# Q2 of the second group by seven 256x256 products: making its weights a group earlier, and the last product's later

## The chip, the cores and the metric

The kernel runs on 1 core of a Trainium2 chip. The metric is the device time of one execution in microseconds (us), as the median of several runs. Lower is better. TensorE (PE) multiplies, VectorE (DVE) and ScalarE (ACT) work on vectors, GpSimd (POOL) sets up, and SyncE (SP) issues nearly all transfers.

## What is computed

`x` holds 64 items of 64 rows by 1024 (4096 rows of 1024 in all). Each item is first multiplied by one of 16 small matrices, then goes through a gated low-rank layer with 64 experts of rank 16, and is added to `x`:

```python
def cond(x, condition, weights):
    return jnp.einsum('bct,bcd->bdt', x, weights[condition])

def ffn(x, A, B, Wr):                      # xf: 4096 rows of 1024
    scores = xf @ Wr.T
    top_vals, top_idx = jax.lax.top_k(scores, 16)
    G = jnp.zeros((N, 64)).at[jnp.arange(N)[:, None], top_idx].set(softmax(top_vals))
    h = jnp.einsum('nd,krd->nkr', xf, A)
    return 2 * jnp.einsum('nkr,kdr->nd', h * G[:, :, None], B)

out = x + ffn(cond(x, cond, W), A, B, Wr)
```

With A and B laid flat these are two products of 4096x1024 by 1024x1024, with gates and a softmax over the 16 best of 64 scores between them.

## The kernel before

**Numbers.** Everything is fp32. For TensorE an operand is split into a high and a low part in a faster type (`fp32r`): ScalarE casts the high part (`hi`, a CAST), VectorE subtracts it from the source to get the low part (`lo`). Three matmuls (high by high, high by low, low by high) stand for one.

**Groups and products.** The 4096 rows are worked in four groups of 1024 (`s` = 0 to 3, `NS`). In each, both large products are done in seven block products instead of eight (Strassen's scheme in Winograd's form). The first half of a group makes P2, P1, P5, P3, P6, P7, P4 (`FIRST`, m = 0 to 6), each in four tiles (j = 0 to 3) of twelve matmuls, one bank of `Pb` per tile. The text calls them tiles 0 to 27 of the group: tile 4m + j. ScalarE copies the results of P2, P1, P5 and P3 out of their banks, VectorE adds up P1, P6, P7 and P4 (`drain_first`). For s > 0 it does this two banks at a time, after the second and the fourth tile. The next product may write a bank only after that. The second half makes Q2, Q1, Q6, Q7, Q4, Q5, Q3 (`SECOND`).

**Products of 256x256.** Some of the products of the second half are themselves done in seven products of 256x256 blocks (`TWO`, by group). Such a product takes 84 matmuls of 256 columns (`two`, line 693) instead of 48 of 512 (`second`, line 674). It needs seven combinations of its input instead of four parts (`FORMS`; four of them are sums by `sums_two`, all seven are split into high and low), and seven combined weights instead of four. Before, Q4 (m = 4) and Q3 (m = 6) are done so from the second group (s = 1) on, Q2 (m = 0) from the third (s = 2) on.

**Made weights.** The seven combined weights of such a product are made once, in the shadow of TensorE's work, from raw blocks of B that lie in SBUF, are stored to `Wd` in HBM, and are loaded from there like all other weights. `MADE_AT` gives the tile at which each of the seven is made and `MADE_IN` the group. At such a tile ScalarE casts the high part into a staging place (`made_hi`), VectorE subtracts the low part (`made_lo`) and after the second, third and fourth does one, two and one sums on the raw blocks in place, and SyncE stores the place at the following tile (`made_store`). A staging place can be cast into again only when its store has landed (`stored`). Before, the weights of Q4 are made in the second half of the first group, those of Q3 at tiles 0, 2, 4, 6, 12, 13, 15 of the second group from the block in `raws[2]` (part of `BR`), those of Q2 at tiles 0 to 6 of the third group, from the same place, which is loaded again with B[0, 0] at tile 18 of the second group. The staging places are the two halves of `xc` (elsewhere the places of x on its way to the small products) and the two halves of `u`.

**Who waits for whom.** The order on each engine is written out by hand in the order of tiles, and each engine works strictly in it. For one tile ScalarE does: the high splits for the next product, `made_hi`, the softmax pieces and score copies, the copy of the banks. VectorE does: the low splits, `made_lo`, the sums T1 to T4 (`sum_t3` at tile 13), the pieces of top 16 (`top_a`, `top_b`, `top_c`), the gates (`gated`), the drain. SyncE does: the weight load for nine tiles ahead (`weights_load`), the store of a made weight, the loads of x for the output (`q_load`, tiles 8 to 15), and at tiles 16 and 20 the small matrices. TensorE turns the gates (`T<-idn,G`) before tiles 12 and 20, when VectorE has finished them. All transfers but a few at the start are issued by SyncE and run on one queue.

## Time and profile before

| | before |
|---|---|
| time, median of 3 runs | 710.89 us (710.61 to 710.94) |
| the profiled execution | 710.62 us, of it span 708.7 us |
| PE busy | 703.5 us (99%), granted clock 1.00 |
| DVE busy | 551.6 us (78%) |
| ACT busy | 274.3 us (39%) |
| transfers | 202.89 MB, mean 286 GB/s |

The span is the time from the first to the last instruction that the profiler recorded; the time of an execution has some 1.9 us more around it. The busy share of an engine is an average over all stages. The granted clock is that of TensorE as a share of full speed. The four groups begin at 9.6, 196.8, 371.1 and 544.6 us, and their second halves at 105.9, 282.1, 456.4 and 630.0.

### The profile page before, as it was taken

Reading aid. Unit: us, or ns where it says so; the run is one execution under the profiler, and the core shown is the slowest. Engines: PE = TensorE matmul, PEld = TensorE weight load, DVE = VectorE, ACT = ScalarE, POOL = GpSimd, SP = SyncE. Lnnn points to the kernel's source line nnn. Section 1 sums busy time; section 2 is a strip of 40 time slices with the busy share of each in tenths; the row PEclk is TensorE's granted clock in tenths of the full one; section 3 lists DMA queues with packets and bytes.
Section 4 is the critical chain, followed back from the end, with each engine's and each line's share of the span. In section 5 each row is a group of like instructions: output and inputs, shape, how many; then the busy total and the mean of one; then the engine's idle time right before and its main releaser. Section 6 shows DMA issues by size and latency. Waiting matters only on the chain.

```text
span 708.7 us, 10694 instructions
## 1 busy us (share of the span) xinstructions
PE 703.5 (99%) x3698; PEld 605.1 (85%) x3698; DVE 551.6 (78%) x991; ACT 274.3 (39%) x505; POOL 1.6 (0%) x6
## 2 busy tenths in 40 slices
PE   9999999999999999999999999999999999999998
PEld 8888888888888888888998888898999888888897
DVE  5898999997757796866675868897677296889985
ACT  5675553535436441133333642232333363222220
POOL 0000000000000000000000000000000000000000
PEclk9999999999999999999999999999999999999999
DMA  9976689747899988476899974967679787565686
GB/s 321 406 296 277 216 282 393 284 184 289 337 381 399 324 328 276 173 239 209 326 331 415 364 293 161 311 248 269 221 295 372 264 304 265 180 232 192 234 322 238
DMA packets 63671, 202.89 MB, mean 286 GB/s; under 512 B 10050, under 2 KB 12738, under 8 KB 62978
## 3 DMA queue, kind: packets, MB, share of 16 engines
q1 hardware_dynamic: 61842, 199.06, 76.3%
q10 hardware_dynamic: 1776, 3.15, 1.3%
q8 instruction: 30, 0.49, 0.3%
q14 instruction: 23, 0.19, 0.1%
HBM read 145.03 MB, written 57.15 MB: 285 GB/s over the span
## 4 chain that ended last, share of the span: by engine, by line
PE 98%; DVE 1%; issue 0%; POOL 0%; DVEq 0%; POOLq 0%
PE Pb L654 43%; PE Pb L687 31%; PE Pb L708 10%; PE Cb L636 8%; PE S L719 4%; PE T L726 1%; PE T L767 0%; PE T L773 0%; DVE Q L1031 0%; PE Pb L670 0%; PE Cb L732 0%; DVE Cq L1031 0%; PE T L732 0%; PE S L732 0%; DVE Op L1031 0%
## 5 line engine op out<-in xcount | busy, mean ns | idle before, releaser
L654 PE MATMUL Pb<-Op,Wt 128*128 128x512 f32 x960 | 231.6, 391 | 0.0
L654 PEld LDWEIGHTS Pb<-Op,Wt 128*128 128x128 f32 x960 | 178.9, 188 | 36.6
L687 PE MATMUL Pb<-Wt,Op 128*128 128x512 f32 x684 | 165.4, 392 | 0.0
L687 PEld LDWEIGHTS Pb<-Wt,Op 128*128 128x128 f32 x684 | 127.0, 188 | 25.9 <-DVE Op L1031 0.4
L1031 DVE TENSOR_TENSOR Q<-Pb,Q 128x512 f32<-128x512 f32 (+1 forms) x114 | 100.9, 901 | 34.9 <-issue 23.5
L855 ACT COPY R<-Cb 128x512 f32<-128x512 f32 x60 | 35.1, 588 | 131.2 <-PE Cb L636 131.0
L1031 DVE TENSOR_TENSOR Op<-R,Op 128x512 fp32r<-128x512 f32 x97 | 64.2, 684 | 27.6 <-ACT Op L805 27.6
L654 PE MATMUL Pb<-Ox,Wt 128*128 128x512 f32 x324 | 81.7, 390 | 0.0
L654 PEld LDWEIGHTS Pb<-Ox,Wt 128*128 128x128 f32 x324 | 60.5, 188 | 12.4
L687 PE MATMUL Pb<-Wt,Ox 128*128 128x512 f32 x276 | 69.5, 391 | 0.0
L708 PE MATMUL Pb<-Wt,Op 128*128 128x256 f32 x516 | 65.5, 284 | 0.3
L708 PEld LDWEIGHTS Pb<-Wt,Op 128*128 128x128 f32 x516 | 63.6, 191 | 1.2 <-issue 0.6
L805 ACT CAST Op<-R 128x512 fp32r<-128x512 f32 x97 | 56.1, 622 | 16.2 <-DVE R L1031 9.3
L805 ACT CAST Op<-Cq 128x512 fp32r<-128x512 f32 x72 | 43.2, 621 | 47.7 <-DVE Cq L1031 32.0
L687 PEld LDWEIGHTS Pb<-Wt,Ox 128*128 128x128 f32 x276 | 51.4, 188 | 10.6 <-DVE Ox L1031 0.2
L1031 DVE TENSOR_TENSOR Op<-Cq,Op 128x512 fp32r<-128x512 f32 x72 | 48.6, 682 | 14.8 <-ACT Op L805 14.8
L1031 DVE TENSOR_TENSOR Cq<-Pb,Cq 128x1024 f32<-128x1024 f32 (+1 forms) x40 | 40.2, 1006 | 24.7 <-issue 16.6
L997 ACT COPY Cq<-Pb 128x1024 f32<-128x1024 f32 (+1 forms) x40 | 33.8, 844 | 44.4 <-issue 39.8
L636 PEld LDWEIGHTS Cb<-wbd,xc 128*128 128x128 f32 x384 | 46.4, 191 | 1.6
L636 PE MATMUL Cb<-wbd,xc 128*128 128x128 f32 x384 | 46.7, 275 | 0.0
L1031 DVE TENSOR_TENSOR Cq<-Cq,SG 128x512 f32<-128x512 f32 x64 | 43.2, 683 | 0.0
L1031 DVE TENSOR_TENSOR R<-R 128x512 f32<-128x512 f32 (+2 forms) x29 | 38.5, 1327 | 0.0
(102 smaller groups left out, 575.0 us busy)
## 6 DMA issues: line engine op xcount, KB each, us to landing
Wt<-Wd SPq DMA_DIRECT2D x192, 512.0 KB, 5.5
Wd<-Wt SPq DMA_DIRECT2D x56, 512.0 KB, 4.8
Q<-in_x SPq DMA_DIRECT2D x32, 512.0 KB, 5.4
xc<-in_x SPq DMA_DIRECT2D x24, 512.0 KB, 4.9
out<-Q SPq DMA_DIRECT2D x8, 1024.0 KB, 4.5
out<-Q SPq DMA_DIRECT2D x13, 512.0 KB, 6.1
BR<-in_B SPq DMA_DIRECT2D x4, 1024.0 KB, 7.8
Wd<-xc SPq DMA_DIRECT2D x8, 512.0 KB, 7.6
```

Of the source, the lines that this page charges most:

```text
L636: t = e.matmul(Cb[:, b, 128 * c:128 * c + 128], src[:, 512 * a + 128 * c:512 * a + 128 * c + 128], wbd[:, i, :], start=True, stop=True)
L654: t = e.matmul(Pb[:, j, :], Wt[:, k, a, 128 * c:128 * c + 128], part((USES1[m], s, c), z), start=fresh and (c, a, z) == (0, 0, 0), stop=(c ...
L687: t = e.matmul(Pb[:, i, :], part((USES2[m], s, c), a)[:, 128 * i:128 * i + 128], Wt[:, k, z, :], start=fresh and (c, a, z) == (0, 0, 0), s ...
L708: t = e.matmul(Pb[:, BANK2[k], 256 * i:256 * i + 256], part((USES2[m], s, k), a)[:, c, 128 * i:128 * i + 128], Wt[:, at, z, 256 * c:256 * ...
L719: t = e.matmul(S[:, :], WrT[:, 4 * a + c, :], part((name, s, c), z), start=begin and (c, z) == (0, 1), stop=not begin and (c, z) == (3, 0))
L726: e.matmul(T[:, 0, :], sS[:, 0:128], sS[:, 0:128], start=True, stop=True)
L805: e.copy(part((name, s, c), 0), source(name, s, c)).then_inc(a_hi, 1)
L855: e.copy(R[:, i // 4, 4 * a:4 * a + 4, 128 * (i % 4):128 * (i % 4) + 128], Cb[:, (v + 1) % 2, :].rearrange("p (c n) -> p c n", n=128)).the ...
L997: e.copy(Cq[:, {"P2": 1, "P1": 0, "P5": 3, "P3": 2}[name], j + 1 - n:j + 1, :], Pb[:, j + 1 - n:j + 1, :]).then_inc(a_prod[name], n)
L1031: e.tensor_tensor(to, one, two, op).then_inc(on, n)
```

## The change

Q2 is done by seven 256x256 products in the second group too (`TWO[1]` gets a 0). Its weights are therefore made in the second group, at tiles 1, 2, 3, 5, 6, 7 and 12, in three staging places: both halves of `xc` and `SG`, which holds the gates. Their raw block B[0, 0] is loaded into `u` near the end of the first group, at step 26 of its second half, instead of into `raws[2]` at tile 18 of the second group. The weights of Q3 are made after them, at tiles 13, 14, 15, 20, 21, 22 and 23, from `raws[2]`, staged in `xc` and `u`. The third group makes no weights. The waits are rewritten to go with this: the copy of the third pair of gates into `SG` waits for the store of Q2's sixth weight.

```diff
--- before.py
+++ after.py
@@ -20,8 +20,8 @@
 SENT = -3.4028234663852886e38
 
 
-TWO = [(), (4, 6), (0, 4, 6), (0, 4, 6)]
-LEVEL = (4, 6, 0)
+TWO = [(), (0, 4, 6), (0, 4, 6), (0, 4, 6)]
+LEVEL = (4, 0, 6)
 
 USED = [[*range(28)] + [n for m in range(7) for n in (
     range(56 + 7 * LEVEL.index(m), 63 + 7 * LEVEL.index(m)) if m in TWO[s] else range(28 + 4 * m, 32 + 4 * m))]
@@ -46,10 +46,9 @@
 SUMS2 = ["t1", "t2", "t3", "t4"]
 
 
-
 MADE = [0, 6, 1, 4, 2, 3, 5]
-MADE_AT = {4: [16, 17, 20, 21, 22, 23, 24], 6: [0, 2, 4, 6, 12, 13, 15], 0: [0, 1, 2, 3, 4, 5, 6]}
-MADE_IN = {4: 0, 6: 1, 0: 2}
+MADE_AT = {4: [16, 17, 20, 21, 22, 23, 24], 0: [1, 2, 3, 5, 6, 7, 12], 6: [13, 14, 15, 20, 21, 22, 23]}
+MADE_IN = {4: 0, 0: 1, 6: 1}
 
 HEAD = [(0, 0, 0), (0, 0, 1), (1, 0, 0), (1, 0, 1), (2, 0, 0), (0, 1, 0), (1, 1, 0), (2, 0, 1), (3, 0, 0), (2, 1, 0),
         (3, 1, 0), (3, 0, 1)]
@@ -361,23 +360,27 @@
         def weight2(m, k):
 
             c, n = [(0, 0), (1, 0), (1, 1), (0, 0), (0, 1), (1, 0), (1, 1)][k]
-            return (u if m == 4 else raws[2])[:, 2 * c:2 * c + 2, 256 * n:256 * n + 256]
+            return (raws[2] if m == 6 else u)[:, 2 * c:2 * c + 2, 256 * n:256 * n + 256]
 
         def made(m, n):
 
 
             if m == 4:
                 return raws[1 - n % 4 // 2][:, 2 * (n % 2):2 * (n % 2) + 2, :].rearrange("p a n -> p (a n)")
-            if n % 4 > 1:
+            if m == 0 and n % 3 == 2:
+                return SG[:, :, :].rearrange("p a n -> p (a n)")
+            if m == 6 and n % 4 > 1:
                 return u[:, 2 * (n % 2):2 * (n % 2) + 2, :].rearrange("p a n -> p (a n)")
-            return xc[:, n % 2, :]
+            return xc[:, n % 3 if m == 0 else n % 4, :]
 
         def made_before(m):
             return 7 * LEVEL.index(m)
 
         def stored(m, n):
 
-            return o_made[n % 4], 16 * (n // 4 + 1 + LEVEL.index(m) * (1 if n % 4 == 3 else 2))
+            k = n % 3 if m == 0 else n % 4
+            ahead = {4: (0, 0, 0, 0), 0: (2, 2, 2, 1), 6: (5, 4, 4, 1)}[m][k]
+            return o_made[k], 16 * (ahead + n // (3 if m == 0 else 4) + 1)
 
         def made_part(m, n, a):
             return made(m, n)[:, 512 * a:512 * a + 512].rearrange("p (c n) -> p c n", n=256)
@@ -496,7 +499,7 @@
 
             def made_store(m, n):
                 e.wait_ge(v_made, made_before(m) + n + 1)
-                e.dma_start(Wd[UNITS + 7 * LEVEL.index(m) + MADE[n]], made(m, n)).then_inc(o_made[n % 4], 16)
+                e.dma_start(Wd[UNITS + 7 * LEVEL.index(m) + MADE[n]], made(m, n)).then_inc(stored(m, n)[0], 16)
 
             def cond_weights(s, half):
                 e.load(which_regs, cnd[0:1, 16 * s + 8 * half:16 * s + 8 * half + 8])
@@ -514,7 +517,8 @@
                     e.wait_ge(p_cond, rows_number(s, i - 2, 0))
                 elif s > 1:
                     e.wait_ge(p_cond, rows_number(s - 1, 6 + i, 0))
-                    e.wait_ge(*stored(6 if s == 2 else 0, 4 + i))
+                    if s == 2:
+                        e.wait_ge(*stored(6, 4 + i))
                 else:
                     e.wait_ge(*operand_used(*LAST_XO[NO + 4 + k]))
                 e.dma_start(xc[:, k, :], xf[128 * n:128 * n + 128, :]).then_inc(l_xc[k], 16)
@@ -561,10 +565,6 @@
                         for k in (6, 0):
                             if s == MADE_IN[k] and step - 1 in MADE_AT[k]:
                                 made_store(k, MADE_AT[k].index(step - 1))
-                        if (s, step) == (1, 18):
-
-                            e.wait_ge(v_made, 14)
-                            e.dma_start(raws[2].rearrange("p a b -> p (a b)"), B[0, 0]).then_inc(l_b[4], 16)
                         if s == 0 and 6 <= step < 10:
                             q = 9 - step
                             e.wait_ge(a_rows, max(rows_all(0, q // 2, 0), rows_all(0, q // 2, 1)))
@@ -597,6 +597,10 @@
                         weights_load(BASE[s] + USED[s].index(UNITS + 7 * LEVEL.index(m) + i if m in TWO[s] else 28 + 4 * m))
                         if s == 0 and step - 1 in MADE_AT[4]:
                             made_store(4, MADE_AT[4].index(step - 1))
+                        if (s, step) == (0, 26):
+
+                            e.wait_ge(v_made, 7)
+                            e.dma_start(u[:, :, :].rearrange("p a b -> p (a b)"), B[0, 0]).then_inc(l_b[4], 16)
                         if s == 0 and m < 6:
                             unit_store(32 + step)
                         k = cond_step(s, m, i)
@@ -806,27 +810,25 @@
 
             def made_hi(m, n):
 
-                if n >= 4:
-                    e.wait_ge(*stored(m, n - 4))
+                if n >= (3 if m == 0 else 4):
+                    e.wait_ge(*stored(m, n - (3 if m == 0 else 4)))
+                elif m == 4:
+                    e.wait_ge(v_wlo, 48 if n < 2 else 52)
+                elif m == 0 and n < 2:
+                    e.wait_ge(l_b[4], 16)
+                    if n == 0:
+
+                        e.wait_ge(v_wlo, UNITS)
+                        for k in range(3, 7):
+                            e.wait_ge(*stored(4, k))
+                    e.wait_ge(p_cond, rows_number(1, 6 + n, 0))
                 elif m == 0:
-
-                    e.wait_ge(*stored(6, n + 4 if n < 3 else 3))
-                    e.wait_ge(l_b[4], 16)
-                    e.wait_ge(v_lo["S4"], split_done("S4", 1, 6))
-                    if n < 2:
-                        e.wait_ge(p_cond, rows_number(2, 6 + n, 0))
-                elif m == 6 and n > 1:
-                    e.wait_ge(v_made, 7)
-                elif m == 6 and n == 0:
-
-                    e.wait_ge(v_wlo, UNITS)
-                    for k in range(3, 7):
-                        e.wait_ge(*stored(4, k))
-                    e.wait_ge(p_cond, rows_number(1, 6, 0))
-                elif m == 6:
-                    e.wait_ge(p_cond, rows_number(1, 6 + n, 0))
+                    for q in range(4):
+                        e.wait_ge(v_gate[q], 4)
+                elif n < 2:
+                    e.wait_ge(*stored(0, (6, 4)[n]))
                 else:
-                    e.wait_ge(v_wlo, 48 if n < 2 else 52)
+                    e.wait_ge(v_made, 14)
                 if n > 2:
                     e.wait_ge(v_wsum, 4 * LEVEL.index(m) + n - 2)
                 e.copy(made_part(m, n, 0).bitcast(F32R), weight2(m, MADE[n])).then_inc(a_made, 1)
@@ -982,6 +984,8 @@
                             h = 2 * s + (m > 3)
                             e.wait_ge(p_gturn, h + 1)
                             if s:
+                                if h == 2:
+                                    e.wait_ge(*stored(0, 5))
                                 e.wait_ge(v_gate[3 if h % 2 else 0], 4 * s)
                             elif h == 0:
                                 e.wait_ge(v_wr, 1)
@@ -1138,9 +1142,8 @@
                 e.wait_ge(v_gate[3], 4 * s + c + 1)
                 if s == 0:
                     e.wait_ge(v_t3, 1)
-                elif s < 3:
-                    e.wait_ge(*stored(6 if s == 1 else 0, 6 if c < 2 else 3))
-                    e.wait_ge(v_lo["S4"], split_done("S4", s - 1, steps(s - 1, 6) - 1))
+                elif s == 1:
+                    e.wait_ge(*stored(6, 6 if c < 2 else 3))
                 else:
                     e.wait_ge(v_lo["S4"], split_done("S4", s - 1, 6))
                 add(s2_place(s, c), Cq[:, 0, c, :], Cq[:, 3, c, :], v_s2, ALU.subtract)
```

**SyncE, end of the first group and tiles 0 to 6 of the second.** `out<-Q` are stores of the output, `Wt<-Wd` weight loads (512 KB), `Wd<-BR`, `Wd<-xc`, `Wd<-u` and `Wd<-SG` stores of made weights. Before:

```order
L499 DMA Wd<-BR 128x1024 [waits v_made] x2
L529 DMA out<-Q 128x2x512 [waits v_out] x2
L490 DMA Wt<-Wd 128x1024 [waits o_t5,o_t7,p_second]
L490 DMA Wt<-Wd 128x1024 [waits o_t6,o_t8,p_second]
L490 DMA Wt<-Wd 128x1024 [waits o_t7,o_t0,p_second]
L490 DMA Wt<-Wd 128x1024 [waits o_t8,o_t1,p_second]
L490 DMA Wt<-Wd 128x1024 [waits o_t0,p_first]
L499 DMA Wd<-xc 128x1024 [waits v_made]
L490 DMA Wt<-Wd 128x1024 [waits o_t1,p_first]
L490 DMA Wt<-Wd 128x1024 [waits o_t2,p_first]
L499 DMA Wd<-xc 128x1024 [waits v_made]
L490 DMA Wt<-Wd 128x1024 [waits o_t3,p_first]
```

and now:

```order
L502 DMA Wd<-BR 128x1024 [waits v_made] x2
L533 DMA out<-Q 128x2x512 [waits v_out]
L603 DMA u<-in_B 128x2048 [waits v_made]
L533 DMA out<-Q 128x2x512 [waits v_out]
L493 DMA Wt<-Wd 128x1024 [waits o_t5,o_t7,p_second]
L493 DMA Wt<-Wd 128x1024 [waits o_t6,o_t8,p_second]
L493 DMA Wt<-Wd 128x1024 [waits o_t7,o_t0,p_second]
L493 DMA Wt<-Wd 128x1024 [waits o_t8,o_t1,p_second]
L493 DMA Wt<-Wd 128x1024 [waits o_t0,p_first]
L493 DMA Wt<-Wd 128x1024 [waits o_t1,p_first]
L502 DMA Wd<-xc 128x1024 [waits v_made]
L493 DMA Wt<-Wd 128x1024 [waits o_t2,p_first]
```

The load of B (`u<-in_B`, 1 MB) stands between the two output stores; the first store of a made weight follows one weight load later than it did.

**ScalarE, tiles 12 to 15 of the second group.** The casts `xc<-BR`, `xc<-u`, `u<-BR` make weights, `S` and `T` are the scores, `Cq<-Pb` copies two banks of P3, the casts from `R` are splits of T2. Before:

```order
L805 CAST Ox<-R 128x512 [waits v_t2,p_first] x2
L832 CAST xc<-BR 128x512 [waits v_wsum,o_made0]
L974 COPY sS<-S 128x512 [waits p_sturn,p_score]
L805 CAST Ox<-R 128x512 [waits v_t2,p_first]
L832 CAST xc<-BR 128x512 [waits v_wsum,o_made1]
L980 COPY sc<-T 128x256 [waits v_top,p_sturn]
L997 COPY Cq<-Pb 128x1024 [waits v_lo_S4,p_first]
L805 CAST Ox<-R 128x512 [waits v_t2,p_first]
L832 CAST u<-BR 128x512 [waits v_wsum,o_made2]
```

and now:

```order
L809 CAST Ox<-R 128x512 [waits v_t2,p_first] x2
L834 CAST xc<-u 128x512 [waits v_wsum,o_made0]
L976 COPY sS<-S 128x512 [waits p_sturn,p_score]
L809 CAST Ox<-R 128x512 [waits v_t2,p_first]
L834 CAST xc<-BR 128x512 [waits o_made0]
L982 COPY sc<-T 128x256 [waits v_top,p_sturn]
L1001 COPY Cq<-Pb 128x1024 [waits v_lo_S4,p_first]
L809 CAST Ox<-R 128x512 [waits v_t2,p_first]
L834 CAST xc<-BR 128x512 [waits o_made1]
L834 CAST u<-BR 128x512 [waits v_made]
```

At tile 12 Q2's last weight is cast into xc's first half; at tile 13, behind the score copy and one split, Q3's first weight is cast into the same half and waits for the store (`o_made0`). Behind it stand the copy of the scores and that of P3's banks.

**VectorE, tiles 13 to 15 of the second group.** `xc<-BR` and `u<-BR` are splits of made weights, `R<-R 128x2048` is the sum T3, then T4; `BR<-BR` are sums on raw blocks. Before:

```order
L1031 TENSOR_TENSOR xc<-BR,xc 128x512 [waits a_made]
L1031 TENSOR_TENSOR R<-R 128x2048 [waits v_lo_y12]
L1031 TENSOR_TENSOR Ox<-R,Ox 128x512 [waits a_hi]
L1031 TENSOR_TENSOR sc<-T,sc 128x256 [waits a_sc]
L1165 MAX m<-sc 128x8 [waits v_top]
L1165 MAX m<-sc 128x8 x3
L1168 TENSOR_SCALAR nm<-m 128x4 [waits v_top]
L1031 TENSOR_TENSOR u<-BR,u 128x512 [waits a_made]
L1031 TENSOR_TENSOR R<-R 128x2048 [waits v_t2]
```

and now:

```order
L1035 TENSOR_TENSOR xc<-BR,xc 128x512 [waits a_made]
L1035 TENSOR_TENSOR R<-R 128x2048 [waits v_lo_y12]
L1035 TENSOR_TENSOR Ox<-R,Ox 128x512 [waits a_hi]
L1035 TENSOR_TENSOR xc<-BR,xc 128x512 [waits a_made]
L1035 TENSOR_TENSOR BR<-BR 128x2x256 [waits v_wlo]
L1035 TENSOR_TENSOR sc<-T,sc 128x256 [waits a_sc]
L1168 MAX m<-sc 128x8 [waits v_top]
L1168 MAX m<-sc 128x8 x3
L1171 TENSOR_SCALAR nm<-m 128x4 [waits v_top]
L1035 TENSOR_TENSOR u<-BR,u 128x512 [waits a_made]
L1035 TENSOR_TENSOR BR<-BR 128x2x256 [waits v_wsum,v_made]
L1035 TENSOR_TENSOR BR<-BR 128x2x256 [waits v_wsum]
```

The sum T4 follows the last of these rows. The split ahead of T3 is now that of Q3's first weight, and between T3 and T4 stand four operations more: a split and a sum at tile 14, two sums at tile 15.

## Rows read from the trace of the kernel before

**Rows 1.** The page's busy times, and the granted clock in 40 slices.
```profile
PE 703.5 (99%) x3698; PEld 605.1 (85%) x3698; DVE 551.6 (78%) x991; ACT 274.3 (39%) x505; POOL 1.6 (0%) x6
...
PEclk9999999999999999999999999999999999999999
```

**Rows 2.** Busy time by stretch: window, length, PE, PEld, DVE, ACT, POOL, clock, DMA, GB/s.
```profile
196.80:282.10 85.30, 85.30 (x385) 70.59 (x385) 62.53 (x132) 34.42 (x62) 0.00 (x0) 1.00 0.94 343
371.10:456.40 85.30, 85.30 (x386) 70.57 (x385) 65.19 (x137) 32.97 (x60) 0.00 (x0) 1.00 0.84 312
434.60:456.40 21.80, 21.80 (x99) 18.03 (x97) 17.41 (x25) 7.13 (x13) 0.00 (x0) 1.00 0.77 265
629.90:641.20 11.30, 10.87 (x86) 10.34 (x85) 10.92 (x18) 0.06 (x1) 0.00 (x0) 1.00 0.81 278
```

**Rows 3.** The chain that ended last, in order of time: start, us, what.
```profile
217.18 16.38 PE Pb L654 x72
...
243.54 16.38 PE Pb L654 x72
...
260.35 21.80 PE Pb L654 x96
282.14 8.16 PE Pb L687 x36
...
456.45 4.31 PE Pb L708 x36
...
462.55 5.77 PE Pb L708 x48
```

**Rows 4.** VectorE in order of time, second group: start, us, instruction, count, idle before.
```profile
218.60 1.22 DVE L1031 TENSOR_TENSOR Cq<-Pb,Cq 128x1024 f32<-128x1024 f32 x1 [2.71 <-ACT Cq L997]
...
226.24 1.22 DVE L1031 TENSOR_TENSOR Cq<-Pb,Cq 128x1024 f32<-128x1024 f32 x1
...
242.16 0.68 DVE L1031 TENSOR_TENSOR xc<-BR,xc 128x512 fp32r<-128x512 f32 x1
242.76 2.29 DVE L1031 TENSOR_TENSOR R<-R 128x2048 f32<-128x2048 f32 x1
245.41 0.69 DVE L1031 TENSOR_TENSOR Ox<-R,Ox 128x512 fp32r<-128x512 f32 x1 [0.36 <-ACT Ox L805]
...
257.13 1.22 DVE L1031 TENSOR_TENSOR Cq<-Pb,Cq 128x1024 f32<-128x1024 f32 x1
```

**Rows 5.** SyncE's transfers in order of issue: start, us of issuing, count.
```profile
193.68 4.85 SPq L529 DMA_DIRECT2D out<-Q  x2
...
222.71 0.32 SPq L490 DMA_DIRECT2D Wt<-Wd  x1
...
238.30 0.32 SPq L499 DMA_DIRECT2D Wd<-xc  x1
```

**Rows 6.** Issues at 193.68, 222.71 and 238.30: size, us to landing.
```profile
out<-Q SPq DMA_DIRECT2D x1, 512.0 KB, 11.5
...
Wt<-Wd SPq DMA_DIRECT2D x1, 512.0 KB, 4.7
...
Wd<-xc SPq DMA_DIRECT2D x1, 512.0 KB, 4.2
```

**Rows 7.** DMA by stretch: window, length, TensorE's clock, DMA share, GB/s.
```profile
210.00:220.00 10.00, 1.00 1.03 417
220.00:230.00 10.00, 1.00 1.01 388
230.00:240.00 10.00, 1.00 0.99 381
```

**Rows 8.** ScalarE in order of time, second group: start, us, instruction, idle before.
```profile
204.39 0.62 ACT L832 CAST xc<-BR 128x512 fp32r<-128x512 f32 x1 [8.29 <-DMA Wd<-BR]
...
205.44 1.01 ACT L997 COPY Cq<-Pb 128x1024 f32<-128x1024 f32 x1
...
241.41 0.62 ACT L832 CAST xc<-BR 128x512 fp32r<-128x512 f32 x1
```

## Prediction

> **What bounds the kernel now.** I read the busy shares first, then the clock, then the chain of waits. TensorE is busy 703.5 of 708.7 us at the full granted clock [rows 1], and both first halves that the change touches, those of the second and of the third group, show TensorE busy 85.30 of 85.30 us [rows 2]. So the time is the sum of the matmuls, plus whatever makes TensorE wait. A removed matmul counts in full; work on another engine costs nothing until it makes TensorE late. The chain of waits in order of time [rows 3] gives the start of each tile: I count tiles 0 to 27 in a first half, each 2.73 us.
>
> **Q2 by seven products.** In the second group 36 matmuls of 512 columns take 8.16 us, 0.227 each, so the 48 of Q2 take 10.9 us. In the third group, where Q2 is already made of seven products, 36 and 48 matmuls of 256 columns take 4.31 + 5.77 = 10.08 us [rows 3]. Gain: 0.8 us. This is all that the change can gain by its purpose. A measurement of this kernel can tell about 0.2% from no change, 1.4 us, so a clean success would read as no change.
>
> **What goes with it at nothing.** The extra splits and the four sums for t1 to t4 (5 VectorE operations more in the last eight tiles, others beside the seven products) now fall in the second group as they fall in the third, where VectorE is busy 17.41 of 21.80 us in the last eight tiles and TensorE never waits [rows 2]. The second group has five operations of made weights there as well: 5 x 0.60 = 3.0 us more (0.60 is the distance between starts in [rows 4]), 20.4 of 21.8. That still fits; if it did not, the first products of Q2 would be late. Three more weight loads of 512 KB and the last product's four late stores go into a stretch that has lost its own 1 MB load of B: at nothing. The third group loses 11 VectorE operations and 7 stores; since TensorE is busy 85.30 of 85.30 us there, it gains nothing.
>
> **The queue of transfers at the head of the second group.** Here the change adds. One load of B (1 MB, as two transfers of 512 KB) is now issued between the two output stores at 193.68 and 198.14 us, and seven stores of made weights stand in tiles 1 to 13 where five stood. What the transfers are worth is seen from the landings: the output store issued at 193.68 landed 11.5 us later, at 205.2; the weight load issued at 222.71 landed after 4.7, at 227.4 [rows 5, 6]. By the order of issues it is the 17th behind that store, so one transfer of 512 KB takes 22.2 / 17 = 1.31 us and the queue never empties between; the bytes agree, DMA's share is 1.01 to 1.03 there and still 0.99 at 230 to 240 us [rows 7]. Counting on, the store of xc issued at 238.30 is the 28th: 205.2 + 28 x 1.31 = 241.9, and it landed at 242.5 [rows 5, 6]. So there is no slack in which four transfers more could be made up before tile 13. The store of the seventh made weight of Q2, which is issued in that very place, becomes the 32nd: **205.2 + 32 x 1.31 = 247.1 us**, where the old one landed at 242.5 and nobody waited for it soon.
>
> **Who waits for the stores now.** Before, no cast of made weights waited for a recent store. Now the places are used again at once. (a) The fourth cast (tile 5) waits for the first store, the tenth behind 205.2: 218.3 us. Behind it VectorE has the split, a sum and the drain of P1, which would start at 218.3 + 0.62 + 0.60 + 0.60 = 220.1 instead of 218.60 [rows 4]. The operations from there to the next drain are as many as before, so that one ends at 227.46 + 1.5 = 228.9; TensorE wants its bank at tile 10, 217.18 + 4 x 2.73 = 228.1 [rows 3, 4]. Stall: 0.8 us. (b) The cast of the last product's first weight stands at tile 13, one tile behind the cast whose store it waits for, since both use xc's first half. ScalarE stands until 247.1, where its cast of the same tile ran at 241.41 before [rows 8]. Queued behind it on ScalarE are the scores' copy and the copy of P3's first two banks, which ends near 248.9; TensorE wants that at tile 16, 249.0 + 0.8, so this alone just holds. Queued behind it on VectorE is everything: the split of that weight, then the sum T3.
>
> **The sum on VectorE from tile 13 to P6's first drain.** Before: T3's sum starts at 242.76, one idle stretch of 0.36 at 245.41, and the drain starts at 257.13 and ends at 258.35 [rows 4]; TensorE starts tile 20 at 260.35 [rows 3], 2.0 us later. Now T3's sum starts at 247.1 + 0.62 + 0.60 = 248.3, 5.5 later; less the idle 0.36; and there are four operations more (split and sum at tile 14, split and two sums at tile 15, less the one split that stood there), 4 x 0.60 = 2.4. The drain ends at 258.35 + 5.5 - 0.36 + 2.4 = 265.9, and tile 20 starts 5.5 us late. This holds stall (a) and the wait for the gates before tile 20; it is not added to them. After that VectorE catches up within the last eight tiles, as shown above.
>
> **Sum.** -0.8 + 5.5 = +4.7 us. The profiled execution took 710.62 us (span 708.7 and 1.9 around it): 715.3. The median of the runs, 710.89, lies 0.27 above it, so for the median I say **715.6 us**.
>
> **Bounds.** The unknown is when the store for tile 13 lands. From below: in the old trace the store in that place took 4.2 us [rows 6]; issued at about 239.3 it would land at 243.5. From above: two transfers more than I count, or 1.36 us each, give 249. I take the count of 32, since the same count meets the old store within 0.6 us.
>
> At this place the Trainium skill speaks against my number. The page "DMA: Bandwidth & Descriptors", section "Anatomy of one DMA", fits the time of a transfer issued by GpSimd as 2.0 us plus its bytes at 436 GB/s, 3.2 us for one of these, with no term for what is queued before it. The trace disagrees at the head of the group (11.5 us) and comes near it only at 4.2 [rows 6]. By that rule the store would land at 242.5, tile 20 would start about 1 us late, and the sum would be 710.8 against the profiled execution. As a mechanism of this kernel, a store that waits for no transfer before it, it is the first of the rivals, which goes by the row's 4.2 us.
>
> **The rivals.**
> - *The queue drains* (chance 0.18). If transfers go faster when more are waiting, or VectorE's issue is what paces them, the store lands at 243.5. The drain ends at 258.35 + 1.96 - 0.36 + 2.4 = 262.35, 2.0 late: +1.2, 712.1. For it: the landing times fell from 11.5 to 4.2 us over the stretch. Against it: they fell because transfers were issued more slowly than 1.31 us apart, not because one took less; the share stayed at 0.99 or more.
> - *The stores are no wait at all* (0.08), the case on the other side. The decision falls at 241.5: if the store lands by then, VectorE's extra 2.4 us meets exactly the 2.0 of slack and 0.36 of idle, and only the matmuls count: 710.1, and down to 709.9 if the relief in the third group lets something start sooner. Against it: it needs a store in 2.2 us, and no row is below 4.2.
> - *B lands late* (0.08). The first cast of the group ran at 204.39 before, and P2's copy at 205.44 [rows 8]. Now it needs the 1 MB load, which by my count lands at 205.2 + 2 x 1.31 = 207.8. The cast and P2's copy behind it end at 209.4, just before tile 4 starts at 209.5. Every microsecond later stalls tile 4 by as much, and moves everything after: 717 for 1.5 us.
> - *Seven products as in the fourth group* (0.03). There Q2 takes 11.3 us [rows 2] with 0.4 of it idle, since no work of a next group stands between the products. The second group has that work, as the third. It would give back the 0.8: 711.7 with the stores harmless.
> - My forecast has 0.63.
>
> **How the numbers follow.** Slower by over 0.2% means above 712.3: my forecast, late B, and a little of the draining queue, 0.72. Within 0.2%: the rest of that, the harmless stores and the Q2 case, 0.26. Faster by over 0.2% means under 709.5, which is more than all matmuls saved: 0.02. The range runs from 710.6, which leaves out most of the harmless case, to 717.3, two transfers above my count.
>
> **What would show it.** Right: in the profile after, the 256-column matmuls of the second group number 84 more and 48 of 512 columns are gone, PE's busy time falls by 0.8; ScalarE idles for some 5 us before a cast of xc that waits for a store of xc, ending near 247; VectorE idles beside it; TensorE has a gap near 260 in two parts (before the gates' transposes, before tile 20), and a small one near 228; DMA's share is at 1.0 through to 247. Wrong: that cast starts before 244 us, or TensorE has no gap between 255 and 270; then the counting of transfers is what failed. If the gap is there but Q2 too waits for splits, the cover of the last eight tiles was too thin.

## The result, and the profile after

The changed kernel takes 716.97 us (median of 6 runs, 716.41 to 718.21) against 710.62 before (median of 6): ratio 1.0091, 95% interval 1.008 to 1.0101. It is slower, as forecast, and 1.4 us slower than the forecast of 715.6: the rise is 6.35 us where 4.7 were forecast. The profiled execution took 716.88 us (span 715.0), 6.26 over the one before.

The chain of waits of the kernel after, in order of time (start, us, what); the rows before are [rows 3]:

```profile
194.61 13.18 DMA u<-in_B
207.81 0.63 ACT xc L834
...
209.18 9.70 DMA Wd<-xc
...
240.52 5.97 DMA Wd<-xc
246.51 0.63 ACT xc L834
247.17 0.69 DVE xc L1035
247.86 2.20 DVE R L1035
...
265.61 23.68 PE Pb L658 x96
289.28 4.31 PE Pb L712 x36
...
295.38 5.77 PE Pb L712 x48
```

Before, the chain was TensorE alone in this group. Now it runs through three transfers: B's load until 207.81, the first store of a made weight until 218.9, and the store of Q2's seventh weight until 246.51. Tile 20 starts at 265.61 instead of 260.35, 5.26 us late. Then the same 96 matmuls take 23.68 us instead of 21.80, and Q2 takes 4.31 + 5.77 = 10.08 instead of 10.9.

ScalarE in the second group, its casts that waited for a transfer (start, us, instruction, idle before and what ended it); the rows before are [rows 8]:

```profile
207.81 0.62 ACT L834 CAST xc<-u 128x512 fp32r<-128x512 f32 x1 [11.03 <-DMA u<-in_B]
...
218.91 0.62 ACT L834 CAST xc<-u 128x512 fp32r<-128x512 f32 x1 [2.21 <-DMA Wd<-xc]
...
246.51 0.62 ACT L834 CAST xc<-BR 128x512 fp32r<-128x512 f32 x1 [3.05 <-DMA Wd<-xc]
```

VectorE behind the last of them: T3's sum, T4's sum and P6's first drain; before [rows 4] T3's sum and the drain started at 242.76 and 257.13:

```profile
247.78 2.28 DVE L1035 TENSOR_TENSOR R<-R 128x2048 f32<-128x2048 f32 x1
...
255.01 2.28 DVE L1035 TENSOR_TENSOR R<-R 128x2048 f32<-128x2048 f32 x1
...
264.34 1.22 DVE L1035 TENSOR_TENSOR Cq<-Pb,Cq 128x1024 f32<-128x1024 f32 x1
```

TensorE's gaps in the second group stand in the brackets (idle before, and who ended it):

```profile
225.06 4.38 PE L658 MATMUL Pb<-Ox,Wt 128*128 128x512 f32 x18 [0.82 <-DVE Ox L1035]
229.72 5.78 PE L658 MATMUL Pb<-Ox,Wt 128*128 128x512 f32 x24 [0.28 <-DVE Cq L1035]
...
263.27 0.66 PE L777 MATMUL T<-idn,G 128*128 128x128 f32 x4 [1.42 <-DVE G L1197]
265.61 23.68 PE L658 MATMUL Pb<-Op,Wt 128*128 128x512 f32 x96 [1.68 <-DVE Cq L1035]
```

Why 23.68 for 21.80: busy time by stretch (window, length, PE, PEld, DVE, ACT, POOL, granted clock, DMA share, GB/s):

```profile
261.80:263.30 1.50, 0.08 (x2) 0.03 (x1) 1.43 (x5) 0.00 (x0) 0.00 (x0) 1.00 0.95 353
263.30:265.60 2.30, 0.63 (x4) 0.39 (x4) 2.30 (x4) 1.64 (x4) 0.00 (x0) 1.00 0.98 374
265.60:269.60 4.00, 3.99 (x11) 3.14 (x12) 4.00 (x6) 2.58 (x5) 0.00 (x0) 0.57 0.56 190
269.60:272.00 2.40, 2.40 (x12) 1.97 (x11) 2.40 (x5) 0.62 (x1) 0.00 (x0) 1.00 0.32 60
```

TensorE was busy 0.71 us of the 3.8 before tile 20. In the next 4.0 us, with TensorE busy all the time, the granted clock averages 0.57: most of it is the lower of the clock's two levels, 1.2 of 2.4 GHz, and 11 matmuls run where 4.0 us hold 17 at full clock. The page "TensorE: Matmul & The Clock Gate" of the Trainium skill, Part 1, says that the clock falls back after TensorE was idle, and comes back with activity; the trace agrees, with 0.57 after the gaps and 1.00 from 269.60 on.

Not all of the 1.88 us is the clock. TensorE's instructions in order of time, where a start may lie before the end of the matmuls ahead of it, give for tile 12 and tile 20 before:

```profile
233.75 3.00 PE L654 MATMUL Pb<-Op,Wt 128*128 128x512 f32 x12
260.10 22.04 PE L654 MATMUL Pb<-Op,Wt 128*128 128x512 f32 x96
```

and for tile 12 after:

```profile
235.69 3.00 PE L658 MATMUL Pb<-Op,Wt 128*128 128x512 f32 x12
```

In this view the 96 matmuls took 22.04 us before, and in three runs below, where tile 20 also starts after a wait but at full clock, they take 22.05, 22.06 and 22.08. So the slow clock costs 23.68 - 22.05 = 1.6 us, and the other 0.25 us is only the chain's later start of tile 20 before (260.35 instead of 260.10). By the same view tile 12 starts 1.9 us late and tile 20 5.5 us late: the early delay is 1.9 us, more than the 0.82 + 0.28 in the brackets, which leave out a part of each wait.

So -0.8 (matmuls saved) + 5.5 (tile 20 late, 1.9 of it by tile 12) + 1.6 (slow clock) = +6.3 us.

### The profile page after: what moved, and what is told of

Same layout as the page of the kernel before. It is cut to its first block, busy times and chain, and to the rows that moved or that the text cites. A ratio compares the mean times of both kernels' runs of the same rounds, so it can differ in the third digit from the quotient of the medians.

```text
span 715.0 us, 10786 instructions
## 1 busy us (share of the span) xinstructions
PE 705.6 (99%) x3734; PEld 607.1 (85%) x3734; DVE 557.6 (78%) x1003; ACT 275.9 (39%) x508; POOL 1.6 (0%) x6
## 4 chain that ended last, share of the span: by engine, by line
PE 88%; DVE 6%; DMA 4%; issue 1%; SPq 0%; ACT 0%; POOL 0%; DVEq 0%; ACTq 0%; POOLq 0%
PE Pb L658 35%; PE Pb L691 28%; PE Pb L712 12%; PE Cb L640 7%; PE S L723 3%; DMA Wd<-xc 2%; DMA u<-in_B 2%; DVE Cq L1035 1%; DVE R L1035 1%; DVE Op L1035 1%; PE T L730 1%; DVE Ox L1035 1%; DVE Q L1035 0%; DVE xc L1035 0%; PE Pb L674 0%
## 5 line engine op out<-in xcount | busy, mean ns | idle before, releaser
L691 PE MATMUL Pb<-Wt,Op 128*128 128x512 f32 x732 | 175.5, 391 | 0.0
L691 PEld LDWEIGHTS Pb<-Wt,Op 128*128 128x128 f32 x732 | 136.1, 188 | 28.0 <-DVE Op L1035 0.7
L1035 DVE TENSOR_TENSOR Q<-Pb,Q 128x512 f32<-128x512 f32 (+1 forms) x119 | 103.3, 883 | 33.8 <-issue 21.7
L658 PE MATMUL Pb<-Ox,Wt 128*128 128x512 f32 x336 | 85.0, 391 | 1.1 <-DVE Ox L1035 0.8
L1035 DVE TENSOR_TENSOR Op<-R,Op 128x512 fp32r<-128x512 f32 x102 | 67.2, 683 | 24.1 <-ACT Op L809 24.1
L1035 DVE TENSOR_TENSOR Op<-Cq,Op 128x512 fp32r<-128x512 f32 x75 | 51.0, 683 | 20.5 <-ACT Op L809 20.5
L809 ACT CAST Op<-R 128x512 fp32r<-128x512 f32 x102 | 59.0, 622 | 20.2 <-DVE R L1035 13.2
L712 PE MATMUL Pb<-Wt,Op 128*128 128x256 f32 x480 | 61.2, 284 | 0.4 <-DVE Q L1035 0.2
L712 PEld LDWEIGHTS Pb<-Wt,Op 128*128 128x128 f32 x480 | 59.1, 191 | 1.3 <-issue 1.0
L691 PE MATMUL Pb<-Wt,Ox 128*128 128x512 f32 x180 | 46.7, 392 | 0.0
L691 PEld LDWEIGHTS Pb<-Wt,Ox 128*128 128x128 f32 x180 | 33.3, 188 | 6.6
```

Source lines behind the costliest of these rows:

```text
L658: t = e.matmul(Pb[:, j, :], Wt[:, k, a, 128 * c:128 * c + 128], part((USES1[m], s, c), z), start=fresh and (c, a, z) == (0, 0, 0), stop=(c ...
L691: t = e.matmul(Pb[:, i, :], part((USES2[m], s, c), a)[:, 128 * i:128 * i + 128], Wt[:, k, z, :], start=fresh and (c, a, z) == (0, 0, 0), s ...
L712: t = e.matmul(Pb[:, BANK2[k], 256 * i:256 * i + 256], part((USES2[m], s, k), a)[:, c, 128 * i:128 * i + 128], Wt[:, at, z, 256 * c:256 * ...
L809: e.copy(part((name, s, c), 0), source(name, s, c)).then_inc(a_hi, 1)
L1035: e.tensor_tensor(to, one, two, op).then_inc(on, n)
```

## The experiments

Each compares with the kernel before, on the same chip. Each kernel is the change with something altered, so the time to compare its own with is 716.97 us. The change itself was not run again beside them; the kernel before has medians of 710.46 to 710.68 in these comparisons and 710.62 beside the change, so differences to 716.97 are good to about 0.2 us at best.

**One cause at a time at tile 13.** First, Q2's seventh weight earlier:

```diff
-MADE_AT = {..., 0: [1, 2, 3, 5, 6, 7, 12], 6: [13, 14, 15, 20, 21, 22, 23]}
+MADE_AT = {..., 0: [1, 2, 3, 5, 6, 7, 9], 6: [13, 14, 15, 20, 21, 22, 23]}
```

> Q2's seventh weight is made at tile 9 instead of 12, so that its store has landed before tile 13; nothing else moves. If the late store holds VectorE (theory): no wait of ScalarE at tile 13, T3's sum some 3.1 us earlier than 247.78, P6's first drain ends near 262.5 instead of 265.56, tile 20 waits only some 0.4 us, the clock stays at 1.00 and the 1.9 us at half clock are not paid: about 712.0 us. If the extra VectorE work of tiles 14 and 15 alone is to blame (rival): no change from 716.9.

Measured 712.63 us, ratio 1.0026 (1.0016 to 1.0036). No cast waits at tile 13, T3's sum starts at 244.46, TensorE's gap before tile 20 is 0.71 us where 0.4 was expected, and the clock stays at 1.00:

```profile
262.75 22.05 PE L658 MATMUL Pb<-Op,Wt 128*128 128x512 f32 x96 [0.71 <-DVE Cq L1035]
```

Without the wait for the store the kernel is 4.3 us faster than the change, 1.6 of it the clock that did not fall. VectorE's extra work alone cannot be the cause.

Second, Q3's second and third weight later, the store left as it is:

```diff
-MADE_AT = {..., 6: [13, 14, 15, 20, 21, 22, 23]}
+MADE_AT = {..., 6: [13, 18, 19, 20, 21, 22, 23]}
```

> Q3's second and third weight are made at tiles 18 and 19 instead of 14 and 15, so that four VectorE operations (2.4 us) and one more leave the stretch before P6's first drain; the late store at tile 13 stays. Theory: the wait at tile 13 stays (ends near 246.5), the drain ends some 3 us earlier, near 262.6, tile 20 waits under 1 us more than the other delays: 712 to 713 us, clock at 1.00. Rival (the store alone is the cause, VectorE would have made up its work): a small gain, 716.

Measured 714.63, ratio 1.0055 (1.0039 to 1.0072). The cast of tile 13 still waits until 246.71, the drain starts at 261.28 instead of 264.34, and the clock stays at 1.00. That is as expected, but the time is 1.6 us above the range: the five operations now stand where VectorE has little room. TensorE has new gaps of 0.47, 0.21 and, in Q2, of 0.97 us:

```profile
289.82 1.67 PE L712 MATMUL Pb<-Wt,Ox 128*128 128x256 f32 x12 [0.97 <-DVE Q L1035]
```

Either edit alone brings tile 20 forward by about 3 us and keeps the clock at 1.00 in the profiled execution: its lateness and the fall of the clock needed both, the late store and the extra work ahead of the drain. The gain of 2.3 us, though part of it is the clock, is more than the rival's 0.9.

Both edits together:

> Both edits. Theory: the stretch before tile 20 has slack again, and what is left is the early delay of 1.8 us by tile 13 (TensorE gaps near 224 and 229) less the 0.8 us of matmuls saved: 711.6 us, no gap near tile 20, clock 1.00. If the early delay is made up too: 709.9.

Measured 711.92, ratio 1.0018 (1.0009 to 1.0028), no gap near tile 20. It is 1.2 us over the kernel before, and the trace still has TensorE's gaps of 1.13 and 0.31 us near 226 and 231: the early delay is left. The profiled execution, 712.80, is the slowest of ten, and its second group began 0.6 us later than before. The rival (early delay made up) falls.

**The placement without the product.** `TWO[1]` back to (4, 6), all placements as in the change:

> Q2 of the second group stays at 48 matmuls of 512 columns; only the making of the weights is moved as in the change. If the placement is the whole cost and the product the whole gain: 0.8 us slower than the change, 717.7 us, with the same gaps near 224, 229, 262 and 264 and the same fall of the clock. If the seven products cost something too (splits, sums beside the late drains): at or below 716.9.

Measured 718.08, ratio 1.0104 (1.0087 to 1.0121), with the fall of the clock. It has the same gaps, but of 0.27, 0.28, 2.27 and 1.68 us. The placement is the whole cost. That the product alone makes the difference of 1.1 to the change is not shown: four executions run from 717.43 to 718.96, and in the profiled one the second group began 0.46 us later than in the change (197.09 against 196.63), before anything that differs between the two.

**What sets the landings.** First, B by another queue: `u<-in_B` issued by ScalarE at the same step.

> The change, with the 1 MB load of B issued by ScalarE on its own queue at the same step instead of by SyncE. If the landings are set by all bytes that are under way (theory: one rate for all, whatever the queue): B lands some microseconds before 207.8, but the first store of a made weight still lands near 218 and the store for tile 13 near 246; the gaps near 224 and 229 shrink by less than 0.5 us, tile 20 starts as late as before and the clock falls: 716.4 to 717. If a place behind B in SyncE's queue is what costs (rival): everything behind it lands some 2.6 us sooner, and the whole is about 2 us faster, 714.5.

Measured 716.27, ratio 1.0074 (1.0058 to 1.0089). The landings are as the theory says (only the gap near 224 shrank by more, from 0.82 to 0.17 us): the cast that waited for B now waits for the last store before it,

```profile
208.11 0.62 ACT L830 CAST xc<-u 128x512 fp32r<-128x512 f32 x1 [11.30 <-DMA Wd<-BR]
```

at 208.11, where the same store had landed by 204.39 before [rows 8]; the cast of tile 5 runs at 218.59 and that of tile 13 at 246.14. B, issued near 189, landed after 9.7 us, long before the 207.8 of the change: it overtakes what SyncE had queued. But its bytes must pass all the same and now delay the others. The Trainium skill, page "DMA: Bandwidth & Descriptors", section "Issuing engines are not separate DMA queues", says that transfers issued by different engines run on the same 16 DMA engines, and that issuing from several saves only the time of issuing; the 716.27 us agree.

Second, fewer transfers before the store of tile 13:

```diff
+                        late = 6 * (s == 1)
-                        if s and 8 <= step < 16:
+                        if s and 8 <= step - late < 16:
```

(and `step - late` for `step` down to the load itself, so the loads of x for the output of the second group come at tiles 14 to 21).

> The change with the eight loads of x for the output in the second group at tiles 14 to 21 instead of 8 to 15, so that five transfers of 512 KB no longer stand before the store that tile 13 waits for. Theory (the store lands by its place in the queue): it lands after some 4.2 us, near 244.7, instead of 246.5; VectorE is 1.8 us earlier, and if that keeps the clock up 1.9 us more are saved: 713.2 to 715.1 us. The cast of tile 5 still waits until 218.9. Rival (its landing has nothing to do with what is queued): unchanged, 716.9.

Measured 712.96, ratio 1.0033 (1.002 to 1.0047), 0.2 below the range. The store, issued at 240.97 with the DMA engines half idle (share 0.50 in the 1.4 us before), landed after 3.1 us, so that the cast hardly waited:

```profile
244.07 0.62 ACT L835 CAST xc<-BR 128x512 fp32r<-128x512 f32 x1 [0.19 <-DMA Wd<-xc]
```

In the change it took 6.0 us from 240.52. What stands before it in the queue is what made it late, and this second way to take the wait away gives the same gain as the first, 4.0 us. TensorE's gap before tile 20 is 0.71 us again, the clock stays at 1.00, and the 96 matmuls from there take 22.08 us. 3.1 us is also below the 4.2 that I had taken as the least a store takes.

**The early delay.** Q2's weights spread out, Q3's later:

```diff
-MADE_AT = {..., 0: [1, 2, 3, 5, 6, 7, 12], 6: [13, 14, 15, 20, 21, 22, 23]}
+MADE_AT = {..., 0: [1, 2, 3, 6, 7, 8, 10], 6: [14, 18, 19, 20, 21, 22, 23]}
```

> Q2's weights at tiles 1, 2, 3, 6, 7, 8, 10 and Q3's at 14, 18, 19, 20 to 23: the fourth cast comes a tile later, so that it finds the first store landed, and no cast follows a store of its own place by one tile. Theory: the gaps near 224 and 229 shrink from 1.1 to at most 0.4 us, no gap near 262, clock 1.00; 0.8 us of matmuls are saved and some 0.5 us lost: 710.3 us, within 0.1% of the kernel before. Rival (the early delay comes from B's landing at 207.8 alone): the early delay of 1.7 us stays, 711.6 us.

Measured 711.17, ratio 1.0007 (0.9998 to 1.0016). The first cast still waits for B until 207.96, yet the gaps near 224 and 229 are gone; what is left of them is that the 48 matmuls of tiles 8 to 11 take 11.34 us instead of 11.04. The fourth cast now runs at 219.26 without a wait. So the early delay comes from the placement of the casts and not from B's late landing alone. Whether the wait for the first store makes it, or VectorE's operations that moved a tile later with the casts, this run does not separate. The time is 0.9 us over what I expected, because of a gap of 0.64 us in Q2, at 286.30: VectorE is busy 15.00 of 15.00 us from 275 to 290 there.

> The spread placement and B on ScalarE's queue. Theory: nothing waits for the first cast any more; no gap in the second group: 709.9 us, 0.8 under the kernel before. Rival: B's bytes still delay the stores that the casts wait for: as the spread placement alone.

Measured 711.18, ratio 1.0009 (1.0 to 1.0018), as the rival says and 1.3 us over the theory: with the spread placement, B's queue makes no difference.

**The clock.** Six matmuls into the free bank T in the first of the two gaps:

```diff
+                            if (s, m) == (1, 4):
+                                e.wait_ge(v_top, 10 * h + 3)
+                                for i in range(6):
+                                    e.matmul(T[:, :, :].rearrange("p a n -> p (a n)"), WrT[:, 0, :],
+                                             WrT[:, 0:4, :].rearrange("p a n -> p (a n)"), start=True, stop=True)
                             e.wait_ge(v_top, 10 * h + 10)
```

> The change, with six matmuls of 512 columns on constants into the free bank T before the gates' transposes at tile 20 of the second group (their result is overwritten). They fill the gap of 1.4 us before the transposes; the wait of 1.7 us behind them stays. Theory (the idle stretch lets the clock fall, and the fall costs 1.9 us over tile 20): clock stays at 1.00 and the time falls to 715.0 us. Rival (the gap of 1.7 us alone is enough, or the fall has another cause): unchanged, 716.9 us.

Measured 715.85, ratio 1.0078 (1.0063 to 1.0094). In the profiled execution (715.41 us) tile 20 starts at 265.81, as late as in the change, and the clock stays up where it had been 0.57:

```profile
265.80:269.80 4.00, 3.99 (x17) 3.30 (x18) 4.00 (x6) 2.59 (x5) 0.00 (x0) 1.00 0.61 206
```

TensorE's 96 matmuls from tile 20 on, there:

```profile
265.81 22.06 PE L658 MATMUL Pb<-Op,Wt 128*128 128x512 f32 x96 [1.68 <-DVE Cq L1040]
```

The wait of 1.68 us behind the transposes is still there, so in this execution that wait alone did not make the clock fall. In the profiled executions, work that nobody needs makes the kernel 1.5 us faster. By the medians it is 1.1, less than the 1.9 expected, and the intervals of the two ratios overlap a little. It is no certain cure: of its four runs the slowest, 716.87, has a mean clock of 0.998, the others 0.999 to 1.0. In the other profiled executions the clock fell at tile 20 in those with both gaps (this change, the placement without the product, B on ScalarE's queue) and in none of the rest. The run with B on ScalarE's queue shows the scatter within one kernel: 715.05 us at a mean clock of 1.0, 716.05 and 716.49 at 0.998, 717.61 at 0.995. The last is the profiled one, and there the clock costs 24.79 - 22.05 = 2.7 us after gaps as long as in the change:

```profile
265.23 24.79 PE L654 MATMUL Pb<-Op,Wt 128*128 128x512 f32 x96 [1.68 <-DVE Cq L1034]
```

**Towards a better version.** With u's halves as the first places of Q3's weights and xc's after them (seven lines, not shown: the place, the semaphore of `stored`, three waits), Q3's first weight needs no recent store and can be made in VectorE's idle stretch before tile 13:

```diff
-MADE_AT = {..., 0: [1, 2, 3, 5, 6, 7, 12], 6: [13, 14, 15, 20, 21, 22, 23]}
+MADE_AT = {..., 0: [1, 2, 3, 6, 7, 8, 10], 6: [12, 14, 18, 19, 20, 21, 22]}
```

> The spread placement of Q2's weights, and Q3's weights at tiles 12, 14, 18 to 22 with u's halves as its first two places and xc's after them: its first weight is made in VectorE's idle stretch before tile 13 and two operations fewer stand in the last eight tiles. Theory: the gap of 0.6 us that the spread placement has in Q2 at 286 goes, what is left are some 0.3 us near tiles 9 and 10: 710.3 us, 0.3 under the kernel before. Rival (VectorE is full from tile 18 on whatever is moved by one or two): as the spread placement, 711.2.

Measured 710.46 against 710.46 before, ratio 1.0001 (0.9992 to 1.001); the gap in Q2 is gone, as expected, and tiles 8 to 11 still take 0.3 us more than before.

The same with Q3's weights at 12, 13, 14, 18, 19, 20, 21:

> As the run before the last but with Q3's weights at tiles 12, 13, 14, 18 to 21: three more VectorE operations before P6's first drain, three fewer after tile 18. By the spread placement's trace that drain had 1.8 us before tile 20 wanted it, and three operations take 1.8: no gap at tile 20, or one of 0.3 us, and none in Q2: 710.2 to 710.5 us. Rival: VectorE's sum order makes tile 20 late by a microsecond, 711.3.

Measured 710.31 against 710.46, ratio 0.9998 (0.9989 to 1.0007). The trace has no gap in the group, tile 20 and Q2 start where they did before ([rows 3]), and Q2 takes 10.08 us:

```profile
260.34 21.80 PE Pb L658 x96
282.13 4.31 PE Pb L712 x36
...
288.24 5.77 PE Pb L712 x48
```

By the median it is not told apart from the kernel before; it is 0.9% faster than the change. Its profiled execution, 709.65, is the fastest of eleven and reached the second group 0.38 us earlier than the kernel before did (196.25 against 196.63); it has lost that by tile 20, nearly all of it in tiles 8 to 11 (11.34 instead of 11.04 us). So the product's 0.8 us less the placement's 0.4 us would leave about 0.4 us, an estimate from the two traces that the medians (0.15 apart) neither show nor rule out.

Last, this placement without the product:

> The placement of the last run (Q3's weights at 12, 13, 14, 18 to 21), but Q2 of the second group left at 48 matmuls of 512 columns. Theory: this placement costs nothing, the product saves 0.8 us by itself: 0.8 us slower than that run, 711.1 us, Q2 takes 10.9 us instead of 10.1, no gap in the second group. Rival: without the extra splits and sums something else is saved, and the difference is under 0.4 us.

Measured 710.95 against 710.6, ratio 1.0006 (0.9997 to 1.0015). The chain of waits of its profiled execution:

```profile
261.01 21.80 PE Pb L658 x96
282.80 8.16 PE Pb L691 x36
```

Its profiled span, 709.3 us, is 1.4 over that of the run with the product. Two things make it up: tile 20 starts at 261.01 instead of 260.34, and Q2 takes 10.9 us instead of 10.08. The first has nothing to do with the product: the execution was late from its start, with the first of the large products at 9.70 instead of 9.12 us. The medians, each against the kernel before on its chip, lie 0.5 apart and the two intervals of the ratios overlap, so the times alone don't settle the product's gain; the durations of the matmuls give 0.8.

## Why the prediction was right, and where it fell short

- **The matmuls.** Predicted -0.8, measured -0.8 (Q2 in 10.08 us). Right.
- **The queue.** By counting transfers I had B at 207.8, the first store at 218.3 and the seventh weight's store at 247.1. The casts that wait for them run at 207.81, 218.91 and 246.51. The runs with B on another queue and with later loads of x show that it is the bytes ahead that set the landing. Right, with 0.6 us of error at the third. The rival that the queue drains, with its landing at 243.5, fell. Two readings beside it are wrong and changed nothing: two transfers above the count of 32 would land at 249.7, not 249, and give 718.2, not the range's upper end of 717.3; and the kernel before did have a cast that waited for a recent store, the one at 204.39 with 8.29 us [rows 8].
- **The early stall (a).** Predicted 0.8 us at tile 10. There were two, of 0.82 and 0.28 us in the brackets, and tile 12 starts 1.9 us late: the split of T1 that tile 8 needs was late as well, which I had not priced. The price was less than half of what it should be, and it did no harm only because it is contained in VectorE's sum to tile 20. The cause named (the first store) fits the trace: the cast waits until 218.91 for it. The spread placement agrees without proving it.
- **The sum to tile 20.** Predicted: P6's drain ends at 265.9, tile 20 5.5 us late. Measured 264.34 + 1.22 = 265.56 and 5.3 late by the chain, the view that the forecast used. Right.
- **What was missing: the clock.** The text put the time as "the sum of the matmuls, plus whatever makes TensorE wait", and priced a wait at its length. After the two gaps before tile 20 the granted clock fell, and tile 20 onward paid 1.6 us more. That term is the whole shortfall: without it the profiled execution is +4.6, for a forecast of +4.7. The granted clock was 1.00 in every slice of the profile before, and I took that as given for the kernel after too. But there TensorE never paused, while my own sum put it idle for 5.5 - 0.8 = 4.7 us in two gaps close together. The median still lies inside the range of 710.6 to 717.3, by 0.3 us. That is luck: the upper end was drawn for a later store, not for a slower clock, and two of the six runs lie above it.
- **The cover of the last eight tiles.** Predicted to hold, at 20.4 of 21.8 us; in the change it held, with no gap after tile 20. The slow clock gave VectorE more time there, but it also held at full clock, with the six matmuls, where the last eight tiles took 22.06 us. That it is thin was seen when five operations more were put there: gaps up to 0.97 us.
- **The bounds.** The least time of a store was taken as 4.2 us, the nearest row; with little queued before it it took 3.1. From the fit in the Trainium skill, page "DMA: Bandwidth & Descriptors", section "Anatomy of one DMA", which is for transfers issued by GpSimd, comes an estimate of 3.2 for this size. The trace comes near it there, with a store that SyncE issued; queued behind others such transfers took 4.2 to 11.5 us.
- **The signs.** The chain's casts, the gaps and the 36 matmuls more (84 less 48) came as written. PE's busy time did not fall by 0.8 us: it rose from 703.5 to 705.6, since a matmul at half clock counts as busy for longer, and so does a part of each wait. In the run with neither gap nor fall of the clock (Q3's weights at 12, 13, 14, 18 to 21) it is 702.6. DMA's share did not stay at 1.0 to 247: it was 1.04 from 240 to 243 and 0.90 from there to 246.5.
- **A rival's price.** Seven products as in the fourth group (11.3 us instead of 10.08) would have given 710.1 + 1.2 = 711.3 with the stores harmless, not 711.7. Q2 took 10.08, so this rival fell.

## What to carry to other kernels

Before a step is moved to an earlier stage, count the transfers that stand before its own in the queue and multiply by the measured time of one: 1.31 us here, good to 0.6 us over 32 transfers. A staging place that is used again one tile later turns that landing time into a wait of every engine behind it; here taking the wait away gave 4.0 and 4.3 us, in two ways. Do not price a wait of TensorE at its length alone: here gaps of 1.42 and 1.68 us, close together, cost 1.6 us more at the lower clock afterwards, and how much they cost differs from run to run.

## What the runs showed that I had not expected

The clock fell on a stretch of 3.8 us with TensorE busy 0.71 us of it, stood at half for most of the next 4.0 us, and cost 1.6 us; with six matmuls without use in the first gap it did not fall in the profiled execution. The price is not the same in each run: the change ran from 716.41 to 718.21 us with mean clocks of 0.998 to 0.995, where the kernel before ran from 710.59 to 710.94 beside it (up to 0.9 us apart in longer series). And a transfer on a second queue overtakes the first queue's but delays them by its bytes: the store that had landed by 204.39 landed at 208.11 instead.
